# Products of a score item in pairs of equal row counts, and the third expert product one step earlier, in an attention and mixture-of-experts kernel

## The reference

```python
xn = _layernorm(x, axis=-1)
x = x + _L0_attn_ref(xn, ...) + _L0_ffn_ref(xn, ...)

# attention
scores = jnp.einsum('bhqd,bhkd->bhqk', q, k) / math.sqrt(hd)
scores = jnp.where(causal, scores, -jnp.inf)
attn = jax.nn.softmax(scores, axis=-1)
out = jnp.einsum('bhqk,bhkd->bhqd', attn, v)
return out.transpose(0, 2, 1, 3).reshape(b, s, d) @ Wo.T + bo

# experts
top_val, top_idx = jax.lax.top_k(logits, 2)
y_all = jnp.einsum('btd,edm->btem', x, We)
```

## Time and profile before

| | |
|---|---|
| time, median of 3 runs | 514.58 us (512.86 to 516.21) |
| span of the profiled execution | 510.5 us |
| PE busy | 477.8 us, 94% |
| DVE busy | 420.7 us, 82% |
| ACT busy | 396.9 us, 78% |
| POOL busy | 345.9 us, 68% |
| chain that ended last | PE 89%, DVE 3%, ACT 3%, DMA 2%, issue 2% |
| granted clock of PE | full in nearly all slices |

### The profile page before, as it was taken

How to read it: one execution, slowest core, us unless ns; L and a number is a source line. 1 busy time by engine, 2 the same in 40 slices (tenths; PEclk the granted TensorE clock), 3 DMA queues, 4 the chain that set the end, 5 groups by cost and what they waited for, 6 DMA issues and landing times.

```text
span 510.5 us, 17312 instructions
## 1 busy us (share of the span) xinstructions
PE 477.8 (94%) x6274; PEld 393.8 (77%) x6274; DVE 420.7 (82%) x1111; ACT 396.9 (78%) x1062; POOL 345.9 (68%) x561
## 2 busy tenths in 40 slices
PE   2548799999999999999999999999999999999995
PEld 1437688888888888888888888888888888888863
DVE  5897698888888898888888898888888898888721
ACT  3644688888888888888888888888888888887773
POOL 7264657777777777778777777777777777755443
PEclk9999999999999999999999999999999999999999
DMA  4664746656547566655465566655556566552000
GB/s 124 195 140 117 188 122 152 161 136 156 134 119 162 130 151 156 160 139 145 105 168 128 148 154 160 156 141 143 139 128 147 138 152 161 133 132 44 15 13 22
DMA packets 64281, 67.79 MB, mean 133 GB/s; under 512 B 6828, under 2 KB 59180, under 8 KB 59484
## 3 DMA queue, kind: packets, MB, share of 16 engines
q1 hardware_dynamic: 64196, 66.68, 53.0%
HBM read 44.90 MB, written 21.23 MB: 130 GB/s over the span
## 4 chain that ended last, share of the span: by engine, by line
PE 89%; DVE 3%; ACT 3%; DMA 2%; issue 2%; SPq 0%; POOL 0%; DVEq 0%; POOLq 0%; ACTq 0%
PE m L841 23%; PE oT_ps L911 17%; PE scoreT_ps L887 13%; PE score_ps L867 12%; PE scoreT_ps L892 5%; PE score_ps L861 5%; PE m L953 3%; PE m L996 3%; PE m L1014 3%; PE m L926 2%; PE m L1021 1%; PE m L962 1%; DMA qstack<-mT 1%; ACT probs L499 1%; DVE negmax L625 1%
## 5 line engine op out<-in xcount | busy, mean ns | idle before, releaser
L625 DVE TENSOR_REDUCE negmax<-score_ps 128x2 f32<-128x512 f32 (+1 forms) x384 | 249.7, 678 | 46.4 <-PE score_ps L867 43.7
L499 ACT ACTIVATE probs<-scoreT_ps 128x512 f32<-128x512 f32 x384 | 216.5, 603 | 74.2 <-PE scoreT_ps L887 48.0
L394 POOL TENSOR_TENSOR fours<-lower,upper 128x512 f32<-128x512 f32 x64 | 81.7, 1276 | 54.1 <-ACT upper L549 54.1
L841 PE MATMUL m<-we_hl,xnT_hl 128*128 128x512 f32 x384 | 114.6, 420 | 0.0
L867 PE MATMUL score_ps<-kstack,qstack 72*128 72x128 bf16 (+1 forms) x1024 | 103.8, 224 | 5.6 <-DVE negmax L625 5.5
L887 PE MATMUL scoreT_ps<-qstack,kstack 123*128 123x128 bf16 (+1 forms) x1024 | 102.0, 221 | 3.3 <-DMA qstack<-mT 2.6
L911 PE MATMUL oT_ps<-probs,vaug 128*32 128x256 f32 (+1 forms) x2048 | 96.7, 329 | 0.2 <-ACT probs L499 0.2
L887 PEld LDWEIGHTS scoreT_ps<-qstack,kstack 123*128 123x128 bf16 (+1 forms) x1024 | 68.1, 98 | 26.5 <-ACT probs L499 15.4
L911 PEld LDWEIGHTS oT_ps<-probs,vaug 128*32 128x32 f32 x2048 | 57.3, 109 | 29.1 <-ACT probs L499 0.4
L549 ACT ACTIVATE upper<-m,weight 128x128 f32<-128x128 f32 x256 | 73.1, 376 | 8.2 <-PE m L841 8.2
L867 PEld LDWEIGHTS score_ps<-kstack,qstack 72*128 72x128 bf16 (+1 forms) x1024 | 72.1, 100 | 8.8 <-DVE negmax L625 7.6
(11 more groups left out here) (81 smaller groups left out, 649.7 us busy)
## 6 DMA issues: line engine op xcount, KB each, us to landing
kstack<-scratch SPq DMA_DIRECT2D x93, 192.0 KB
scratch<-parts SPq DMA_DIRECT2D x64, 192.0 KB, 2.4
qstack<-scratch SPq DMA_DIRECT2D x62, 192.0 KB
qstack<-scratch SPq DMA_DIRECT2D x31, 256.0 KB
x_sb<-in_x SPq DMA_DIRECT2D x32, 128.0 KB, 2.3
scratch<-parts SPq DMA_DIRECT2D x32, 128.0 KB, 1.9
out<-out_sb SPq DMA_DIRECT2D x32, 128.0 KB, 3.7
qstack<-mT SPq DMA_DIRECT2D x64, 8.0 KB, 2.1
```

Of the source, the lines that this page charges most:

```text
L394: g.tensor_tensor(fours[:, :, q, :], lower[:, :, q, :], upper[:, :, q, :], ALU.add).then_inc(pool_sum, 1)
L499: a.activation(o, i, ACT.Exp, scale=SCALE).then_inc(act_exp, 1)
L625: v.tensor_reduce(o, score_ps[n % 2][:].rearrange("p (h k) -> p h k", h=w), axis=AX.X, op=ALU.max, negate=True).then_inc(dve_max, 1)
L841: ins = tn.matmul(o, l, r, start=first, stop=l is low)
```

## The change

There are two edits, both on PE, and no instruction is added or taken away.

First, in a mixed item the loops over the two heads and over the two halves are exchanged, so that products of one row count stand side by side: a score item takes 72, 72, 123, 123 rows instead of 72, 123, 72, 123; a turned item takes 74, 74, 123, 123 instead of 123, 74, 123, 74. Each product writes the same place as before.

Second, `experts(mix, 2)` is called at step 8, behind the transpositions L996, instead of at step 9 behind S9. So it now stands ahead of T3 and S9.

```diff
                 else:
-                    for c in range(2):
-                        h = head(grp, 2 * (j - 1) + c)
-                        for q, top in ((0, MAX_ROW), (1, ALL_ROWS)):
+                    for q, top in ((0, MAX_ROW), (1, ALL_ROWS)):
+                        for c in range(2):
+                            h = head(grp, 2 * (j - 1) + c)
                             ins = tn.matmul(ps[:, c * S + q * P:c * S + (q + 1) * P], qs[0:top, h, P:S],
                                             ks[0:top, h, q * P:(q + 1) * P], start=True, stop=True)
...
                 if j < 2:
-                    for c in range(2):
-                        h = head(grp, 2 * j + c)
-                        for q, top in ((0, ALL_ROWS), (1, MAX_ROW + MAX_PARTS)):
+                    for q, top in ((1, MAX_ROW + MAX_PARTS), (0, ALL_ROWS)):
+                        for c in range(2):
+                            h = head(grp, 2 * j + c)
                             ins = tn.matmul(ps[:, c * S + q * P:c * S + (q + 1) * P], ks[0:top, h, 0:P],
                                             qs[0:top, h, q * P:(q + 1) * P], start=True, stop=True)
...
-                    if n == 9 and has(s, -1):
+                    if n == 8 and has(s, -1):
                         pe.wait_ge(dve_lower, upto(mix, per=2, k=1))
                         experts(mix, 2)
```

## The result

| | before | changed |
|---|---|---|
| time, median | 513.88 us (4 runs, 512.86 to 516.21) | 533.06 us (4 runs, 531.60 to 534.41) |
| ratio | | 1.036, 95% interval 1.033 to 1.039 |
| span of the profiled execution | 510.5 us | 530.8 us |
| PE busy | 477.8 us, 94% | 487.0 us, 92% |
| first L996, and period of a turn | 65.7 us, 14.41 us | 68.1 us, 15.0 us |

The change makes the kernel 3.6% slower; 3.0% was forecast, and 533 us lie inside the range of 523 to 535.

The account below looks back on a forecast made before the run. PE's program was taken to bound the kernel; 27 turns x 0.52, 3 x 0.45 and 0.2 for the last made +15.6 us, on the median of 514.58 giving 530 us, 3.0% slower, range 523 to 535.

Parts of the forecast that it names:

- What bounds the kernel: PE's program sets the time from turn 2 on, 14.4 us a turn, with DVE as late as it may be at L926.
- The pairs: In the 16 mixed items of a turn, fewer row-count changes save 0.006 us each, 0.1 us in all.
- The move's own gain: Expert products placed behind L996 instead of S9 save about 0.06 us a turn on PE.
- The delay: T3 and S9 late behind the 0.79 us expert products, so DVE's o_sb is late, PE waits, L926 starts 0.60 us late.
- Turns 29 to 32: The last turns: 3 x 0.45 = 1.4 us for 29 to 31, which have no L926, and 0.2 for turn 32.
- Turns 0 and 1: At the start PE waits for transfers anyway, so nothing is added.
- PE going past the waiting transpositions: At L1021 PE runs later ready work during the wait, only savings stay: 4.8 us less, 509.8; chance 0.04.
- The time given back: PE's steps behind expert and value products shrink, up to all of 0.52 us a turn goes: 514 to 520; chance 0.08.
- goes on in the next turn: Late ACT and DVE make an item of the next turn wait too, by 0.2 us: 536 us; chance 0.04.
- A pair that saves nothing: In the mixed items pairs give no gain, so a turn costs 0.59 us more: 532 us; chance 0.25.
- serialises: In mixed items equal rows keep a weight load from overlapping the product before, 0.045 us a pair: 573 us; chance 0.01.
- 0.015 us an item: Upper bound of the pairs' saving in each mixed item, giving 528 us; no chance of its own.

Follow-up runs that it names:

- move_only: The kernel before with the third expert product at step 8 and no pairs; 536.10 us, ratio to before 1.040.
- behind_t3: The changed kernel with the third expert product between T3 and S9 instead of ahead of T3; 534.95 us, ratio to before 1.037.
- all_123: The changed kernel with the third expert product back at step 9 and all mixed-item products reading 123 rows; 512.72 us, ratio to before 0.995.
- pairs_only: The changed kernel with the third expert product back at step 9, only the pairs left; 513.61 us, ratio to before 0.995.
- joined: Pairs without the move, T6 ahead of L926, L996 between S9 and the third expert product, L1021 behind S11; 523.85 us, ratio to before 1.016.

## Why the prediction was right

**What bounds the kernel** held: in the changed kernel too the period is what PE's program and its waits make it, and it was longer in every one of the 27 turns.

**The pairs** were taken at 0.006 us an item, and the spacings give 7 ns. Outside the window S8 to L926 the change was to save 0.07 us a turn; from L926 to the next L996 it is 11.51 us where it was 11.58, by the ns 0.08 less.

**The move's own gain** was swallowed by the wait, as forecast; its parts came as written (products 0.36 us behind the first transposition, T3 1.15). Its size can be read where no wait has come yet: in `move_only` T4 starts 1.62 us behind L996 where it was 1.66, so it is 0.04 to 0.05 us and not 0.06.

**The delay.** Step by step, in us behind L996, forecast and measured: maxima of S9 1.82 and 1.81; T5 2.24 to 2.25 and 2.24; end of `o_sb` 2.78 and 2.83; L1021 2.84 and 2.89; S11 3.11 and 3.17; L926 3.43 and 3.49. The chain was right and one term was mis-sized: I took 0.55 us from the start of the maxima of S9 to `o_sb`, as in the earlier trace rows, and it was 0.61. In the kernel before, this reduction started under the tail of `rden` and took 0.63; behind a wait it takes 0.69. The better figure stood in the same rows: the two reductions from 252.89 on, of which the first comes behind a wait, take 1.20 us to the start of `rden`, 0.60 each. It is the place behind `rden` that is short, not the wait that is dear. That 0.06 goes through to L926, 0.67 us late against 0.60 forecast. It makes the turn 0.59 longer instead of 0.52, over 27 turns 2 of the 4.7 us by which the span grew more than forecast.

**Turns 29 to 32** were put at 1.6 us and took 2.0 (the distances of L996 there grew by 0.65, 0.48, 0.54 and 0.34).

**Turns 0 and 1** were put at nothing. The span has 2.4 us there, of which most or all is the form of the start. In full: 510.5 + 2.4 + 26 x 0.59 + 2.6 (from the 27th L996 to the end) = 530.8. Without the form of the start the span would have grown by 17.9 us against 15.6 forecast, so the forecast was about 2 us short like against like. The late start, which no term of its sum had, came on top, and the range up to 535 held both.

**The rivals.** PE going past the waiting transpositions: it stands in every turn, and `behind_t3` shows it standing from 267.6 us, when the maxima of S9 had freed S11, to 267.99. The time given back: nothing was, the shift of L926 (0.67) less the 0.08 that the pairs save behind it is the longer turn. By the same sum nothing goes on in the next turn. A pair that saves nothing, or serialises: the second of two equal products follows the first at 58 to 60 ns and the next one follows at 55, where serialised weights would have given 100. (The time that the prediction gives for 0.015 us an item, 528, should be 527: 11 items x 0.009 us x 30 turns are 3.0 less than 530.2.) The Trainium skill's rule ("TensorE: Matmul & The Clock Gate", Part 3, The mechanism) that a weight load overlaps running products only with another row group is not borne out here: in `all_123` every product of these items reads the same 123 rows, and its weight load (98 ns) starts 2 ns behind the start of the product before it, at 55.6 ns a product. The same section also lets a load go ahead into a background weight buffer; these rows agree with that part of it.

## What to carry to other kernels

When two engines are equally late at one point, a block moved ahead of the item on which the other engine's chain begins costs nearly its whole length, less the slack, in each turn (here a block of 0.79 us cost 0.66); look on the other engine for what is queued behind the item you delay, not only for what the moved block itself waits for. Before moving work away from between two dependent items, ask what wait it was covering. When a wait has opened, look for a new order on the waiting side first (the work that nobody needs yet goes last): in this case it took 0.34 us a turn of the loss away, while the place for which the block was moved was worth 0.04 to 0.05. In the kernel before, without the move, that order was not tried.

## What the runs showed of the hardware

**A change of the row count costs one product 3 to 4 ns.** It does so even between 74 and 72 rows, and shows in the spacing that follows the changed product.

**TensorE's clock fell just behind the wait for one transfer.** In turn 2, PE waits for the rows of the maximum. In the kernel before it waited 2.56 us and went on at full clock; in the changed kernel it waited 3.73, and the records behind are longer, those of L911 1.51 us before and 2.79 here. First the changed kernel, then its granted clock (third column from the end) in two stretches of 5 us:

```profile
63.65 0.44 PE L887 MATMUL scoreT_ps<-qstack,kstack 74*128 74x128 bf16 x4 [3.73 <-DMA qstack<-mT]
63.89 0.63 PE L861 MATMUL score_ps<-kstack,qstack 123*128 123x128 bf16 x4
64.45 2.79 PE L911 MATMUL oT_ps<-probs,vaug 128*32 128x256 f32 x32
67.17 0.42 PE L887 MATMUL scoreT_ps<-qstack,kstack 74*128 74x128 bf16 x4
...
60.00:65.00 5.00, 1.35 (x16) 0.95 (x20) 1.25 (x3) 1.20 (x4) 3.45 (x7) 0.88 0.72 176
65.00:70.00 5.00, 5.00 (x68) 3.57 (x61) 2.56 (x7) 2.64 (x7) 2.57 (x5) 0.77 0.80 193
```

PE ran at the lower of its two levels, 1.2 GHz, from 63.8 to 67.3 us by the granted clock, and the products of S6 start 107 ns apart instead of 55. The fall comes after the wait, 0.2 us into T0. Here the longer wait (3.73 us) went with another 1.3 us at L911, but the length of the wait does not settle it: `pairs_only` waited 3.05 us and went on at full clock, `joined` waited 2.49 and fell at 65.4 us, 1.3 us behind its T0.

**The clock column can miss a stretch.** At 47 us the kernel before shows four products in 0.63 us, where 0.39 is usual, started 107 ns apart, with a clock of 1.00 in the column. The trace has no record of the clock before 47.9 us. So an early stretch is better judged by the length of a known group:

```profile
47.09 0.63 PE L861 MATMUL score_ps<-kstack,qstack 123*128 123x128 bf16 x4
```
